# Causal attention: the heads' copy ahead of the exponentials, and an opening whose loads are spread over three queues

## The reference

```python
gate_x = sigmoid(block_diag_linear(x, w_in, b_in))       # 8 blocks of 32 x 32
gate_a = sigmoid(block_diag_linear(x, w_a, b_a))
a = minimum(exp(-gate_a * (softplus(a_param) + MIN_DECAY)), 1 - EPS)
h = closed_form_rnn_scan(x * gate_x * sqrt(maximum(1 - a * a, EPS)), a)
x = layernorm(x + h)
...
q = frac_rope(einsum('btm,mhd->bhtd', x, wq)) * 128 ** -0.5    # 2 heads of 128
k = frac_rope(einsum('btm,mhd->bhtd', x, wk)) * 128 ** -0.5
s = einsum('bhid,bhjd->bhij', q, k) - NEG * less(i, j)
o = einsum('bhij,bhjd->bhid', softmax(s), v)
x = layernorm(x + einsum('bhid,hdm->bim', o, wo))
```

## Time and profile before

| | us |
|---|---|
| median of 3 runs (1661.14, 1661.80, 1669.12) | 1661.8 |
| the profiled execution, its own time | 1667.65 |
| its span, first to last instruction | 1665.9 |
| TensorE busy | 1527.8 (92%) |
| VectorE busy | 1140.6 (68%) |
| ScalarE busy | 801.7 (48%) |
| GpSimd busy | 578.7 (35%) |

### The profile page before, as it was taken

The page is one execution under the profiler, slowest core; times in us unless marked ns, Lnnn a source line. Parts: engine busy times, 40 slices in busy tenths (PEclk is TensorE's granted clock), DMA queues, the critical chain, the costliest instruction groups (busy, mean ns, idle before and its releaser), DMA issues.

```text
span 1665.9 us, 34482 instructions
## 1 busy us (share of the span) xinstructions
PE 1527.8 (92%) x12806; PEld 1364.2 (82%) x12806; DVE 1140.6 (68%) x2334; ACT 801.7 (48%) x1527; POOL 578.7 (35%) x679
## 2 busy tenths in 40 slices
PE   3888898899999999788888699999989999999997
PEld 2677777799999999777777578888879999999997
DVE  3899987756655565146777358877867768676775
ACT  5777742244544455236666444545434444443443
POOL 2666651212112120047776211212104444343444
PEclk8999999899999999999999899999999999999999
DMA  5122253212323330152233132121134553635443
GB/s 188 64 77 76 70 189 115 83 39 89 96 95 101 101 102 26 49 200 74 77 91 96 65 124 77 53 78 53 53 73 93 104 121 83 123 85 110 97 92 72
DMA packets 118829, 152.03 MB, mean 91 GB/s; under 512 B 10330, under 2 KB 103716, under 8 KB 118180
## 3 DMA queue, kind: packets, MB, share of 16 engines
q1 hardware_dynamic: 111540, 129.75, 28.4%
q0 software_dynamic: 6144, 16.79, 3.6%
q10 hardware_dynamic: 1008, 3.67, 0.6%
HBM read 111.37 MB, written 38.80 MB: 90 GB/s over the span
## 4 chain that ended last, share of the span: by engine, by line
PE 29%; DVE 11%; issue 7%; DMA 5%; ACT 4%; SPq 1%; POOL 1%; DVEq 0%; ACTq 0%; POOLq 0%
PE psum L518 7%; PE psum L1788 4%; DMA arena_x<-wT_d 3%; PE psum L1772 3%; PE psum L485 3%; PE psum L493 2%; PE psum L1766 2%; DVE psum L2358 2%; PE psum L1749 2%; PE psum L1488 1%; ACT arena_y L1519 1%; DMA wT_d<-arena_w 1%; DVE C_st L437 1%; PE psum L477 1%; PE psum L1485 1%
## 5 line engine op out<-in xcount | busy, mean ns | idle before, releaser
L2129 POOL TENSOR_TENSOR d_g_parts<-arena_w,d_g_parts 128x512 fp32r<-128x512 f32 x128 | 167.8, 1311 | 248.6 <-ACT d_g_parts L2261 240.9
L518 PE MATMUL psum<-d_v_high,d_g_parts 128*128 128x256 f32 x1024 | 205.1, 284 | 4.0 <-POOL d_g_parts L2129 2.3
L518 PE MATMUL psum<-d_x_parts,d_v_high 128*128 128x256 f32 x1024 | 193.5, 287 | 1.7 <-DVE d_x_parts L513 1.7
L518 PE MATMUL psum<-m_w_high,m_h_parts 128*128 128x256 f32 x1024 | 188.0, 285 | 0.0
L1192 ACT ACTIVATE arena_x<-psum,b_e 128x512 f32<-128x512 f32 x128 | 88.2, 689 | 190.1 <-PE psum L518 90.7
L518 PEld LDWEIGHTS psum<-d_v_high,d_g_parts 128*128 128x128 f32 x1024 | 167.5, 190 | 6.5 <-POOL d_g_parts L2129 4.1
L1120 POOL DMA_INDIRECT arena_x<-x_d,slot_row x64 | 66.9, 1045 | 293.6 <-PE psum L1166 229.3
L518 PEld LDWEIGHTS psum<-d_x_parts,d_v_high 128*128 128x128 f32 x1024 | 159.0, 191 | 8.6 <-DVE arena_w L2364 4.1
L518 PE MATMUL psum<-m_xF_parts,m_w_high 128*128 128x512 f32 x512 | 160.2, 395 | 2.1 <-DVE m_xF_parts L513 2.1
L518 PEld LDWEIGHTS psum<-m_w_high,m_h_parts 128*128 128x128 f32 x1024 | 160.9, 192 | 0.0
L2261 ACT ACTIVATE d_g_parts<-arena_w 128x512 fp32r<-128x512 f32 x128 | 80.8, 631 | 153.3 <-DVE arena_w L2364 152.4
(11 more groups left out here) (279 smaller groups left out, 3694.0 us busy)
## 6 DMA issues: line engine op xcount, KB each, us to landing
arena_x<-wT_d SPq DMA_DIRECT2D x128, 256.0 KB, 6.4
arena_y<-in_L_ffn_w SPq DMA_DIRECT2D x16, 1024.0 KB, 7.9
x_d<-arena_x SPq DMA_DIRECT2D x32, 256.0 KB, 2.2
y_d<-arena_x SPq DMA_DIRECT2D x16, 512.0 KB, 9.0
arena_x<-kv_d SPq DMA_DIRECT2D x16, 512.0 KB, 3.3
kv_d<-arena_x SPq DMA_DIRECT2D x9, 512.0 KB, 3.0
arena_x<-in_x SPq DMA_DIRECT2D x16, 256.0 KB, 2.9
arena_x<-in_ctx SPq DMA_DIRECT2D x16, 256.0 KB, 3.2
```

The source lines that it names most:

```text
L518: ins = nc.tensor.matmul(dst, left[a_], right[b_], start=start and k == 0, stop=stop and k == 2, skip_group_check=True)
L2129: nc.gpsimd.tensor_tensor(K["gP"][:, s % 4, 1], K["g"][:, s % 2], K["gP"][:, s % 4, 0].bitcast(F32), ALU.subtract).then_inc(d_gl, 1)
```

## The change

Two things are changed.

The copy of the vectors comes ahead of the mask's, the memset and the identity's cast behind the decay chain, and the three instructions that read tables have gone to `setup_tables`, which VectorE does in step 2 of stage A. The diff, without the moved loads' declarations:

```diff
@@ setup_sync, setup_pool, setup_scalar @@
+            sp.dma_start(const[:, 0:P], a["constants"][:, 0:P]).then_inc(s_const, 16)
+            sp.dma_start(A["x"][:, 0], x_u[0]).then_inc(a_in[0], 16)
             for dst, src in loads:
                 sp.dma_start(dst, src).then_inc(s_const, 16)
             sp.wait_ge(s_zero, 1)
-            for dst, src in diag:
-                sp.dma_start(dst, src).then_inc(s_const, 16)
+            for dst, src in diag[::2]:
+                sp.dma_start(dst, src).then_inc(s_diag, 16)
...
             pool.wait_ge(s_pow, 2)
+            for dst, src in tables_in:
+                pool.dma_start(dst, src).then_inc(s_tables, 16)
+            for dst, src in weights_in:
+                pool.dma_start(dst, src).then_inc(s_weights, 16)
...
+            act.wait_ge(s_zero, 1)
+            for dst, src in diag[1::2]:
+                act.dma_start(dst, src).then_inc(s_diag, 16)
             act.wait_ge(s_vec, 1)
@@ setup_vector @@
+        def setup_tables(dve):
+            dve.wait_ge(s_tables, 16)
             nc.vector.tensor_scalar(kb_par[:, 0, :], vec[:, V_BK:V_BK + 2], table("even_heads"), None,
                                     ALU.mult).then_inc(s_setup, 1)
...
             nc.vector.tensor_copy(causal_bf[:, :], table("causal")).then_inc(s_setup, 1)
...
+        N_DECAY = 5
         N_SETUP = 10
@@ a_sync @@
-                if u0:
+                if u0 and not (u0.fixed and u0.n == 0):
@@ a_tensor @@
+                    if t.fixed and t.n == 1:
+                        pe.wait_ge(s_diag, 16 * len(diag))
...
+                    if t.fixed and t.n == 4:
+                        pe.wait_ge(s_weights, 16 * len(weights_in))
@@ a_scalar @@
-            act.wait_ge(s_setup, N_SETUP)
+            act.wait_ge(s_setup, N_DECAY)
@@ a_vector @@
+                if t.fixed and t.n == 2:
+                    setup_tables(dve)
@@ a_gpsimd @@
+                    if t.fixed and t.n == 2:
+                        pool.wait_ge(s_tables, 16)
@@ c_scalar @@
+                if u3:
+                    done(act, c_o, u3)
+                    done(act, c_wo, u3.back(1))
+                    nc.scalar.activation(C["oF"], chunks(bank(6)), ACT.Copy).then_inc(c_os, 1)
                 if u2:
                     done(act, c_sub, u2)
...
                     ins.then_inc(c_ex, 1)
-                if u3:
-                    done(act, c_o, u3)
-                    done(act, c_wo, u3.back(1))
-                    nc.scalar.activation(C["oF"], chunks(bank(6)), ACT.Copy).then_inc(c_os, 1)
```

More of the change, by code:

```diff
@@ L283, in decoder @@
         slot_row = sb("slot_row", [P, SLOTS // P], I32)
-        s_const, s_zero = sem("s_const"), sem("s_zero")
+        s_const, s_zero, s_diag, s_tables, s_weights = (sem("s_" + n) for n in ("const", "zero", "diag", "tables", "weights"))
         s_vecT, s_vec, s_setup = sem("s_vecT"), sem("s_vec"), sem("s_setup")
@@ L290, in decoder @@
         s_pow = sem("s_pow")
-        loads = [(const[:, :], a["constants"])]
+        loads, tables_in, weights_in = [], [(const[:, P:], a["constants"][:, P:])], []
         vec_src = [("L0_attn_a_param", 2), ("L0_attn_b_in", 2), ("L0_attn_b_a", 2),
@@ L307, in decoder @@
         for name in ("L0_xattn_Wq", "L0_xattn_Wk", "L0_xattn_Wv"):
-            loads.append((w[name][:, :, :], a[name].rearrange("(c p) n -> p c n", p=P)))
-        loads.append((w_route[:, :, :], a["L0_ffn_wg"].rearrange("(c p) n -> p c n", p=P)))
+            weights_in.append((w[name][:, :, :], a[name].rearrange("(c p) n -> p c n", p=P)))
+        weights_in.append((w_route[:, :, :], a["L0_ffn_wg"].rearrange("(c p) n -> p c n", p=P)))
         loads.append((mask_in[:, :], a["mask"]))
-        N_EARLY = len(loads) + len(diag)
+        N_EARLY = 1 + len(loads)
         late = []
@@ L402, in setup_vector @@
             nc.vector.tensor_scalar(mask_f[:, :], mask_in[:, :], -BIG, None, ALU.mult).then_inc(s_maskf, 1)
-            dve.wait_ge(s_maskT, 1)
-            nc.vector.tensor_copy(mask_key[:, :], bank(6)[:, 0:B]).then_inc(s_mask, 1)
             dve.wait_ge(s_vecT, 1)
@@ L408, in setup_vector @@
             nc.vector.tensor_scalar(hgate_b[:, :], vec[:, V_BIN:V_BIN + 4], 0.5, None, ALU.mult).then_inc(s_setup, 1)
+            nc.vector.tensor_scalar(ndecay[:, :], vec[:, V_A:V_A + 2], 0.0, MIN_DECAY, ALU.max,
+                                    ALU.add).then_inc(s_setup, 1)
+            dve.wait_ge(s_maskT, 1)
+            nc.vector.tensor_copy(mask_key[:, :], bank(6)[:, 0:B]).then_inc(s_mask, 1)
+            dve.wait_ge(s_act_setup, 3)
+            dve.wait_ge(s_setup, 2)
+            nc.vector.tensor_tensor(ndecay[:, :], ndecay[:, :], sp_tmp[:, 2, :], ALU.add).then_inc(s_setup, 1)
+            dve.wait_ge(s_setup, 3)
+            nc.vector.tensor_scalar(pdecay[:, :], ndecay[:, :], 0.5, None, ALU.mult).then_inc(s_setup, 1)
+            dve.wait_ge(s_setup, 4)
+            nc.vector.tensor_scalar(ndecay[:, :], ndecay[:, :], -0.5, None, ALU.mult).then_inc(s_setup, 1)
+            nc.vector.memset(mask_one[:, :], -BIG).then_inc(s_setup, 1)
+            nc.vector.tensor_copy(ident_bf[:, :], ident).then_inc(s_setup, 1)
+        def setup_tables(dve):
+            dve.wait_ge(s_tables, 16)
             nc.vector.tensor_scalar(kb_par[:, 0, :], vec[:, V_BK:V_BK + 2], table("even_heads"), None,
@@ L412, in setup_vector @@
                                     ALU.mult).then_inc(s_setup, 1)
-            nc.vector.tensor_scalar(ndecay[:, :], vec[:, V_A:V_A + 2], 0.0, MIN_DECAY, ALU.max,
-                                    ALU.add).then_inc(s_setup, 1)
-            nc.vector.tensor_copy(ident_bf[:, :], ident).then_inc(s_setup, 1)
             nc.vector.tensor_copy(causal_bf[:, :], table("causal")).then_inc(s_setup, 1)
-            nc.vector.memset(mask_one[:, :], -BIG).then_inc(s_setup, 1)
-            dve.wait_ge(s_act_setup, 3)
-            dve.wait_ge(s_setup, 4)
-            nc.vector.tensor_tensor(ndecay[:, :], ndecay[:, :], sp_tmp[:, 2, :], ALU.add).then_inc(s_setup, 1)
-            dve.wait_ge(s_setup, 8)
-            nc.vector.tensor_scalar(pdecay[:, :], ndecay[:, :], 0.5, None, ALU.mult).then_inc(s_setup, 1)
-            dve.wait_ge(s_setup, 9)
-            nc.vector.tensor_scalar(ndecay[:, :], ndecay[:, :], -0.5, None, ALU.mult).then_inc(s_setup, 1)
+        N_DECAY = 5
         N_SETUP = 10
```

## The result

| | before | after |
|---|---|---|
| median of the runs of one comparison (14 each) | 1671.46 us | 1649.63 us |
| the profiled execution, its own time | 1667.65 | 1660.16 |
| its span | 1665.9 | 1658.4 |

The ratio of after to before is 0.9897, with a 95% interval of 0.9877 to 0.9917: on the 1661.8 us of the prediction that is 17.1 us less (13.8 to 20.4), where 18.9 were forecast. One of the 14 executions of the kernel before took 8529.40 us; the ratio leaves it out. So the kernel got faster, by a little less than forecast. In this comparison, though, the kernel before had a median of 1671.46 and not 1661.8; that it has more than one usual time is part of what follows, and compared like with like the gain is 12 to 14 us.

The account below looks back on a forecast made before the run. It took a 12.67 us attention loop through ScalarE, TensorE and VectorE, and SyncE's issue of small loads in the opening, as bounds. 8.4 + 10.5 = 18.9 us off 1661.8 gave 1642.9, forecast as 1643, range 1634 to 1654.

Parts of the forecast that it names:

- The attention round: Attention stage: with the heads' copy before the exponentials, a ScalarE-TensorE loop of 11.94 us sets the round; 11.9 taken, 0.7 off.
- The attention stage: Causal-attention stage: the moved heads' copy is worth 10.5 us in all, bounds 0 and 18.6.
- the thirteen rounds: Attention stage, first heads copy to last exponentials but one: 13 rounds at 0.7 us each, 9.1 us.
- The stage's end: Last attention round: with the copy swapped, the output projection gains 1.4 us, bounds 0 and 3.
- The opening: Kernel start: fewer loads gate it, so TensorE's first instruction comes at 6.8 instead of 15.19; 8.4 us, bounds 6.4 and 9.1.
- last issue to release: Opening: SyncE's last issue ends at 4.90; 1.22 us to release on quiet engines gives 6.1, loaded 8.8; 6.8 taken.
- Rival 1: Opening: small loads share the DMA engines with tables and weights and land only with them; gain 5.6, total 1645.7; chance 0.15.
- The later waits: After the opening's semaphore: waits for gate blocks (slack 1.4 us), tables, weights and router are covered and cost nothing.
- rival 4: Opening: GpSimd's slow DMAs land tables past 18.9, losing each microsecond beyond; at 27.3 the time is 1651.3; chance 0.04.
- The microseconds arrive at the end: Stages after the two stretches: they wait only on each stretch's end, so all 18.9 us reach the total.
- The base: Whole kernel: the median time before the change, 1661.8 us, from which the 18.9 us were subtracted.
- rival 3: Attention stage: exponentials stuck behind the copy while TensorE's clock is lower; five such rounds give 1671.9 us; chance 0.03.

Follow-up runs that it names:

- v_copy_later: The changed kernel with ScalarE's copy of v moved behind the next round's copies of x3 and of the scores; ratio to before 0.9850.
- the two pairs: Profiles of before and after (1667.65 and 1660.16 us), then of the same two kernels again, unedited (1663.45 and 1649.23 us).
- opening_only: The kernel before with only the opening half of the change, the heads' copy staying behind the exponentials; ratio to before 0.9970.
- tables_late: The changed kernel with GpSimd starting tables and weights only after identity, vectors and mask have landed; ratio to before 0.9913.
- tables_last: The changed kernel with GpSimd's tables and weights held until identity, vectors, mask and all sixteen gate blocks have landed; ratio to before 0.9882.

## Why the prediction was right or wrong

- **The attention round** was right in its mechanism and in the loop: 11.9 was forecast, from legs of 11.94, and 11.82 measured. Nearly all of the 0.12 is the heads' copy, which holds up the exponentials by 0.49 and not by its whole 0.60. The two things that the profile was to show, the heads' copy released by the value product and no wait ahead of the exponentials, are in the timeline. v_copy_later showed by experiment that this loop sets the round.
- **The attention stage** was forecast at 10.5 and gave 12.4 and 10.4 in the two pairs. Its terms: the thirteen rounds gave 8.9 and 9.0, where 13 x 0.7 = 9.1 was forecast. That is close partly by luck, since the old round was taken as 12.6 throughout and the first three were 12.3 and the last 11.6 (the mean of thirteen is 12.5), while the new one came out 0.1 shorter than forecast. The stage's end gave 4.2 and 2.6, where 1.4 was forecast: mis-sized, and 1.7 of the first pair's goes with the low clock of that one execution of before. The beginning, to which the prediction gave nothing, lost 0.8 and 1.2.
- **The opening** is the step that failed. It said 8.4 with bounds from 6.4, and gave 3.6 and 3.9 in the two pairs and 5.0 in opening_only. The arithmetic of the queue was nearly right (SyncE's last issue ended at 5.7, 4.9 was forecast), but the step "last issue to release" was taken near its quiet end, 1.9 us, since "the big tables leave GpSimd's queue only after its memsets". That was no reason: the memsets end at 1.3 and the tables are under way from 1.7. It took 6.1 in after (5.4 to 6.3 in the five profiles with this opening), and tables_late, with the tables held back, took 1.7: the small loads were waiting beside the large ones. Rival 1 named the mechanism and was given 0.15. It should have been the forecast, for the tables' bytes stood in the bandwidth row and nothing held them back. Its price of 5.6 was too kind as well, because it let the small loads land with the tables at 9.6; in after the tables landed at 10.8 and the mask at 11.75. As for the pages, the Trainium skill ("DMA: Bandwidth & Descriptors", section "Issuing engines are not separate DMA queues") says that the same 16 DMA engines serve all issuers and interleave them. That the trace bears out: the mask lands later beside the tables, on either queue. By its other half, that several issuers save only a small initiation time, the opening would have given about nothing. It gave 3.6 to 5.0 us, and with the tables held back the same three issuers bring the input copy 9 us forward, so here the measurement decides against it.
- **The later waits** (gate blocks, tables, weights) cost nothing in after, as forecast; five loads were through GpSimd's sequencer by 5.3, at 0.74 to 0.78 each, inside the bounds and below the 0.95 that was taken. In tables_last, where they start late, VectorE waits 0.9 us for them, which is rival 4 in small.
- **"The microseconds arrive at the end"** failed in the first pair by 9.1 us and held in the second but for 0.4 (and 1.5 between the input copy and the attention stage, whose place was not looked for). The prediction had named "if later stages lose what these gained" as a break, and had given it no price. It was there to be priced: TensorE waits 4.5 us at that hand-over in before too, and the clock over the two units behind it was 0.79.
- **The total** came out near the forecast by luck as well: 17.1 against 18.9, though the opening gave 3.6 to 5.0 of its 8.4. Like with like it was 12 to 14 us, and the rest is the mix of executions, which the prediction had no term for.
- **The base.** 1661.8 was a median of three. In three later comparisons the kernel before had runs from 1658.0 to 1674.5 and medians of 1667.8 to 1670.0. A forecast in us carries this uncertainty besides its own; one in us saved does not.
- **The slower case** (rival 3) didn't appear: the thirteen rounds stayed at 11.8 us each.

## What to carry to other kernels

When small loads gate the start, hold the large ones back until the small ones have landed; here a second queue for the large transfers didn't take them out of the way. When a copy is moved in an in-order queue, add up the loops it closes: here 12.6 became 11.82 and one more copy moved gave 11.33, near the 11.4 worked out for TensorE alone. And before a few microseconds are read from one pair of profiles, compare the stretches that the edit doesn't touch: the feed-forward stage moved by 6 to 7 us and the cross-attention's start by 4 to 5 between executions of one kernel.

## What the hardware showed that was not expected

- A 4 KB load landed 1.7 us after the end of its issue with no large transfer beside it, 5.2 beside 2.2 MB on ScalarE's queue (one profile), and 5.4 to 6.3 beside the same bytes on GpSimd's (five profiles). With these, SyncE's issue of it took 0.85 to 1.97 us instead of 0.58 to 0.62.
- Loads of 256 KB in the feed-forward stage land in 6.2 to 6.8 us in some executions and 8.8 to 9.2 in others, of the same kernel in two cases.
- After TensorE's wait of 4.5 us the clock was at its lower level for differing lengths of time in the same kernel (granted 0.53 and 0.66 over the two units in the two profiles of after), and at 1.00 when extra matmuls filled the wait.
- After the same wait of 3.1 us in the attention stage's last rounds the granted clock was 0.66 in one execution of the kernel before and 1.00 in the other.
